# Attention source scalars: the last 192 of 832 edge tiles taken by GpSimd gathers from a stored table, the first 640 by the lookup loop

## The reference, cut to what matters

```
al_src = (h * a_src).sum(-1)            # one scalar per node and head
al_dst = (h * a_dst).sum(-1)
e = leaky_relu(al_src[src] + al_dst[dst], 0.2)
alpha = softmax of e over the edges of one dst
out = segment_sum(alpha * h[src], dst)
```

## Time and profile before

| | us |
|---|---|
| three runs | 10758.03, 10766.74, 10762.2 (median 10762.2) |
| profiled execution, its own time | 10761.99 |
| its span | 10760.2 |
| POOL busy | 6324.8 (59%) |
| PE busy | 6118.1 (57%) |
| DVE busy | 5059.5 (47%) |
| ACT busy | 1560.0 (14%) |

### The profile page before, as it was taken

How to read it: one execution, slowest core, us unless ns; L and a number is a source line. 1 busy time by engine, 2 the same in 40 slices (tenths; PEclk the granted TensorE clock), 3 DMA queues, 4 the chain that set the end, 5 groups by cost and what they waited for, 6 DMA issues and landing times. The chain is left out here.

```text
span 10760.2 us, 143680 instructions
## 1 busy us (share of the span) xinstructions
PE 6118.1 (57%) x32219; PEld 5125.3 (48%) x32219; DVE 5059.5 (47%) x17185; ACT 1560.0 (14%) x3639; POOL 6324.8 (59%) x6901
## 2 busy tenths in 40 slices
PE   4555566665555546755777753444555567853333
PEld 4445455554555533535777633333444456733332
DVE  6666755554444421685666633334211115733334
ACT  0000033332000001740000000000221225710000
POOL 6666466775666662106666546664566666646665
PEclk7777778887666668558999965555666768965555
DMA  2111211112333312005666521112655656421111
GB/s 78 43 45 45 59 47 45 45 45 61 90 91 90 91 55 73 4 11 145 185 185 185 165 79 46 46 46 57 147 156 155 159 155 145 151 92 46 46 46 47
DMA packets 651433, 941.53 MB, mean 88 GB/s; under 512 B 253820, under 2 KB 427892, under 8 KB 650812
## 3 DMA queue, kind: packets, MB, share of 16 engines
q0 software_dynamic: 252288, 606.77, 21.1%
q1 hardware_dynamic: 299360, 328.15, 9.9%
q10 hardware_dynamic: 99548, 4.42, 0.8%
HBM read 794.65 MB, written 144.18 MB: 87 GB/s over the span
## 5 line engine op out<-in xcount | busy, mean ns | idle before, releaser
L534 PE MATMUL block_windows<-block_hot,block_message 128*128 128x128 f32 x3328 | 871.1, 393 | 881.3 <-DVE third_acc L458 418.1
L534 PE MATMUL sage_windows<-sage_hot,sage_message 128*128 128x128 f32 x4992 | 959.3, 357 | 584.2 <-DVE sage_hot L402 396.2
L534 PEld LDWEIGHTS sage_windows<-sage_hot,sage_message 128*128 128x128 f32 x4992 | 925.1, 267 | 679.3 <-DVE sage_hot L402 452.7
L534 PEld LDWEIGHTS block_windows<-block_hot,block_message 128*128 128x128 f32 x3328 | 741.0, 286 | 979.9 <-issue 624.2
L2214 POOL DMA_INDIRECT eh_message<-t_q,all_position x896 | 848.5, 947 | 533.3 <-issue 248.0
L387 POOL DMA_INDIRECT block_message<-t_rel,all_src x832 | 789.8, 949 | 576.2 <-issue 209.3
L387 POOL DMA_INDIRECT sage_message<-t_x,all_src x832 | 870.4, 1046 | 425.4 <-issue 217.2
L387 POOL DMA_INDIRECT rgcn_message<-t_rel,all_src x832 | 788.7, 948 | 520.9 <-issue 204.4
L458 DVE TENSOR_TENSOR first_acc<-first_acc,sage_windows 128x128 f32 (+1 forms) x1664 | 588.2, 353 | 1063.9 <-remote 596.6
L387 POOL DMA_INDIRECT block_message<-in_x,all_src x832 | 818.8, 984 | 434.7 <-issue 204.0
L534 PE MATMUL gat_windows<-gat_hot,gat_message 128*128 128x128 f32 x6656 | 901.9, 293 | 287.9 <-issue 207.6
(11 more groups left out here) (474 smaller groups left out, 11739.8 us busy)
## 6 DMA issues: line engine op xcount, KB each, us to landing
eh_window<-t_p SPq DMA_DIRECT2D x896, 64.0 KB
t_hidden<-eh_hidden SPq DMA_DIRECT2D x112, 512.0 KB
sc_rows<-t_hidden SPq DMA_DIRECT2D x112, 512.0 KB
eh_low_rows<-t_low SPq DMA_DIRECT2D x112, 256.0 KB
t_rel<-n_h SPq DMA_DIRECT2D x49, 512.0 KB, 2.6
eh_message<-t_q,all_position POOLq DMA_INDIRECT x896
block_message<-in_x,all_src POOLq DMA_INDIRECT x832
sage_message<-t_x,all_src POOLq DMA_INDIRECT x832
```

The costliest lines, as they stand in the source:

```text
L534: last = nc.tensor.matmul(ps[k][:, b, :], message[u][:, f:f + P], hot[:, u, j * P:(j + 1) * P], start=(j == 0), stop=(j == heads - 1))
```

## The change

The loop runs AITERS = 20 iterations: 160 quads, LOOKED = 640 tiles. The other GOT = 192 tiles are gathered. SP first stores `m.al` to a DRAM table `t_al` of 6272 rows of 16 bytes. POOL, behind its 49 scatters, waits for that store and then issues 192 indirect DMAs, each fetching 16 bytes for 128 edges into `rows_got`; two semaphores take turns every 16 DMAs, and from the third batch on POOL waits at the head of a batch for the batch two before. ACT waits for all of them behind its part of the loop and copies the two source columns to `m.e` in one operation of 128 x 384.

```diff
-    AITERS = T // (AQ * QU)
-    assert T % (AQ * QU) == 0
+    AITERS = 20
+    LOOKED = AITERS * AQ * QU
+    GOT = T - LOOKED
+    assert 0 < GOT and GOT % 16 == 0
...
+        rows_got = sb("rows_got", [P, GOT, 4])
+        got = [sem(f"got{k}") for k in range(2)]
+        table_kept = sem("table_kept")
...
         def _(sp):
+            sp.dma_start(m.t_al.rearrange("(j p) w -> p j w", p=P), table[:]).then_inc(table_kept, 16)
             sp.wait_ge(ints_padded, 2)
...
+            pool.wait_ge(table_kept, 16)
+            for n in range(GOT):
+                batch, turn = divmod(n, 16)
+                if batch >= 2 and turn == 0:
+                    pool.wait_ge(got[batch % 2], 16 * 16 * (batch // 2))
+                pool.indirect_dma_start(rows_got[:, n, :], None, m.t_al,
+                                        bass.IndirectOffsetOnAxis(ap=m.src[:, LOOKED + n:LOOKED + n + 1], axis=0)).then_inc(got[batch % 2], 16)
             pool.wait_ge(placed, 16 * NT)
...
                 keep(AITERS - 1, q)
+            for k in range(2):
+                act.wait_ge(got[k], 16 * sum(1 for n in range(GOT) if n // 16 % 2 == k))
+            nc.scalar.copy(m.e[:, :, LOOKED:T].rearrange("p k t -> p t k"), rows_got[:, :, 0:2])
...
-        m.t_last = table("t_last", TP * P, 4)
+        m.t_last, m.t_al = table("t_last", TP * P, 4), table("t_al", ROWS, 4)
```

## The result

| | before | changed |
|---|---|---|
| median of 4 runs each, side by side | 10763.74 | 10934.83 |
| lowest to highest | 10758.03 to 10766.74 | 10928.09 to 10946.34 |
| profiled execution, its own time | 10761.99 | 10937.53 |
| its span | 10760.2 | 10935.7 |
| POOL busy | 6324.8 (59%) | 6509.8 (60%) |

The ratio is 1.0161, with 95% interval 1.0143 to 1.0178: 171 us slower.

A forecast was written before the change was run, and what follows sets the result against it. ACT's pace of 1.627 us a quad bounds the loop, except while POOL's unbroken indirect DMAs delay PE's signals. Loop +144.8, ACT's copy +0.5, store 0: +145 on 10762 gives 10907 us, range 10860 to 10943.

The forecast's parts named there:

- What holds the loop: In `attention_terms`, PE's signals reach ACT and DVE late while POOL issues indirect DMAs back to back: +144.8 us.
- pauses in POOL's run are where the waits end: In `sage2` and `gat`, waiting engines get PE's signal only once POOL has stopped, 3.25 and 2.08 us idle.
- 48 quads out of the loop, -78.1: In the `attention_terms` loop, 48 quads fewer at ACT's pace of 1.627 us each take 78.1 us off.
- 240.4 us more of POOL: 192 gathers behind POOL's scatters at 1.252 us each add 240.4 us, so POOL ends at 4603.6.
- 22.4 us a quad: Under the gathers, two PE signals per quad at 11.2 us each let 10.7 quads through in 240.4 us.
- The loop resumes 4.85 us after POOL: In `attention_terms`, the loop comes alive 4.85 us behind POOL's last indirect DMA, as behind the 49 scatters.
- rival C: Total holding: no signal passes under the gathers, +163 us, 10925, or 10943 with gathers of 1.35 us; chance 0.09.
- The store, 0, bound 5: The table's store on SP's queue, before edge loads and keys, delays keys 0 to 5 us; taken as 0.
- The cover that the prediction named: The loop is held at its start anyway, hiding the store's delay to the keys; without it 5 us.
- The scaling from the earlier trace: 16384 pieces were used 15.2 us after issue; the store's 6272 are 0.4 of that, at most 5.8 us.
- ACT's copy, 0.5: ACT's last copy, 128 x 384, stands in the open behind the last keep and adds 0.5 us.
- Rival A: Independent engines: gathers hold nothing, the loop resumes at 4368 and ends 77.6 us earlier, time 10684; chance 0.13.

The follow-up runs named there:

- the spaced kernels: Memset of 128x448 before each gather of the changed kernel: 10852.58 us against 10860.26; before each scatter of the kernel before: 10817.09 against 10870.89.
- 209 of them at 1.33 and 1.44 us: Changed kernel with 160 gathers, store on ACT's queue, memset 128x128 or 128x256 before each DMA: 11006.83 and 10960.41 us against 10870.89.
- the kernel with 21 iterations: Changed kernel with 672 tiles looked up, 160 gathered and the table's store on ACT's queue: 11008.01 us against 10860.26 for the kernel before.

## Why the prediction came out right, step by step

*What holds the loop.* The prediction read the earlier trace rows as PE's signals reaching ACT and DVE late while POOL issues indirect DMAs back to back, and put the change's cost there. The trace after and the spaced kernels show this: the hold goes when the DMAs are set apart, on the same kind of chip, and nothing else is touched. Where it said that pauses in POOL's run are where the waits end, the cause was put too simply: POOL need not pause, 1.62 us between DMAs do, and the one step of 2.85 us in the changed kernel's run ended no wait.

*48 quads out of the loop, -78.1.* Right: the pace outside the hold is still 1.627.

*240.4 us more of POOL.* 245.9 us for 191 steps, 1.287 each; the longer steps made it 6.8 us longer, and POOL started 2.4 us later: its end came 9.2 us later than the 4603.6 of the sum.

*22.4 us a quad.* Wrong in size and in its working: 36.4. The prediction took a spacing of 11.2 us from `after_sage2` and let the two signals of a quad follow each other. In the loop each signal waits 66 to 70 us, two quads wait at once, and a quad costs half of a wait and its 3.2 us of work. The rows had signs of it: the waits of the earlier trace rows, 24.7 and 47.3 us, were still growing. It mattered little: the forecast had the loop 12.7 quads behind product 0 at 4608.4, and it was 8 behind it at 4607.27 and 11 at full pace (4641.47). 1.7 quads are 2.8 us.

*The loop resumes 4.85 us after POOL.* This is the step that failed, and the largest miss: 28.7 us (4641.47 - 4612.8), 23.9 more. The earlier trace rows gave 4.85 behind a run of 49. That 241 DMAs simply leave more to drain is not enough, since behind 209 of them at 1.33 and 1.44 us the loop resumed within 1.4 us. Together 23.9 + 9.2 + 2.8 = 35.8 us, the whole distance between the last product's 4846.4 and 4882.20. In the measured time it is 28 (10934.83 against 10907), as the rest of the profiled execution ran 5 us shorter and the median lies 2.7 us under it.

*How much the time confirms.* Little by itself: with most of the loop held for 240 us, any pace of over 20 us a quad gives the same time within 20 us, and total holding (rival C, 10925) lies nearer to 10934.83 than the forecast of 10907. It is the trace with its nine products under the run that tells them apart. That the range held owes something to luck, as the resumption, 23.9 us off, was the largest miss.

*The store, 0, bound 5.* Mis-sized: it delays the first product by 11.4 us here (27.4 behind the first scatter against 16.0 in the earlier trace rows) and 12.2 on a free chip. The cover that the prediction named, the hold, hid it in the pair: by an estimate from the 36.4 us a quad, at most one quad more would have passed. The scaling from the earlier trace rows failed: 16384 pieces took 15.2 us from issue to use there, and these 6272 are on the move for 11.4 us (4302.9 to 4314.3), with the edge loads still to come behind them.

*ACT's copy, 0.5.* 0.85, in the open.

*Rival A* was given 0.13 and judged a property of the program. It is right on every free chip, with 38 us and not 78, for the two terms above. No row of one trace could have told that: the kernel before had one time and one kind of chip in it. The rule of the Trainium skill that spoke for A (Trainium Architecture — The Big Picture, section What this means for kernel authors) agrees with the free chips' traces (0.04 us from a spread's end to ACT) and fails on the holding ones, where PE's signals took 66.0 and 69.6 us.

*Open.* What the DMAs and PE's signals share, and why only some chips show it; why a signal's wait levels off at 66 to 70 us; whether the key loads or SP's signals add to the load. A service time of about 1.40 us per DMA fits the resumption ((4636.66 - 4302.62) / 241 = 1.386; 1.395 in the kernel with 21 iterations) but neither a spacing of 1.44 that still holds nor waits of 53 and 59 us that began when 25 to 28 DMAs were out. That the running loop itself takes a share would help with the first and was only argued. Nor is it shown whether plain DMAs of POOL's hold the loop, since that kernel ran on a free chip alone. The signals to SP, POOL and from DVE were not studied.

## What to carry to other kernels

An engine's stream that looks independent can load something shared: before giving idle POOL a long run of indirect DMAs, look in the trace for late signals under the runs it already has, count how long the hold outlasts the run, and try setting the DMAs apart; here 24 us of memsets bought 54. A store of thousands of 16-byte pieces delayed the loads behind it by over 10 us on either of the two queues tried: put it behind the loads that the next loop starts with. And take a time that stands on one chip as that chip's: this change is worth -38 or +171 us. To find how late a signal is, count the sender's and the reader's instructions and pair them; the nearest sender in time need not be the one waited for.

## What the runs showed of the hardware that was not expected

- The same program takes 9339 or 10764 to 10871 us depending on the chip, with the mean granted clock at 0.72 to 0.73 and at 0.71, too close to make it; the two attention stages with spaced scatters take the same time on both.
- On holding chips PE's signals to DVE and ACT took 66.0 and 69.6 us at 1.25 us between POOL's indirect DMAs, those to ACT 31.8 in the mean at 1.33 and 8.1 at 1.44, and 0.04 us for nearly every quad at 1.62; signals from ACT to PE took 0.05 us at the same time.
- The hold fills and drains: at 1.25 us it outlasts 241 DMAs by 24 to 29 us, at 1.33 and 1.44 it outlasts 209 by 0.6 and 1.4, and after one 2.70 us step of POOL at a spacing of 1.44 it took some 45 us to come back to 8.6 us a quad.
